# Edge values moved from the relu's scale into the destination one-hots, in a graph-attention kernel

## The reference, cut to what matters

```python
scores = jnp.sum(q[dst] * k[src], axis=-1) * scale
scores = scores + (edge_weight[:, None] @ we + be)[:, 0]
seg_max = jax.ops.segment_max(scores, dst, num_segments=n)
exp_s = jnp.exp(scores - seg_max[dst])
denom = jax.ops.segment_sum(exp_s, dst, num_segments=n)
attn = exp_s / jnp.maximum(denom[dst], 1e-12)
out = jax.ops.segment_sum(v[src] * attn[:, None], dst, num_segments=n)
```

## Time and profile before

| | us |
|---|---|
| median of 3 runs (1656.93 to 1661.5) | 1658.9 |
| the profiled execution | 1657.33 |
| its span in the trace | 1655.6 |

### The profile page before, as it was taken

How to read it: one execution, slowest core, us unless ns; L and a number is a source line. 1 busy time by engine, 2 the same in 40 slices (tenths; PEclk the granted TensorE clock), 3 DMA queues, 4 the chain that set the end, 5 groups by cost and what they waited for, 6 DMA issues and landing times.

```text
span 1655.6 us, 40803 instructions
## 1 busy us (share of the span) xinstructions
PE 1505.8 (91%) x9862; PEld 1311.8 (79%) x9862; DVE 1068.7 (65%) x2995; ACT 920.7 (56%) x2928; POOL 724.4 (44%) x1149
## 2 busy tenths in 40 slices
PE   5979999999999999995999999999999979974777
PEld 5968888988988988894888888888888869962444
DVE  7725888888888888885355544555455557985222
ACT  4748999999999999992333333333333334530111
POOL 0046777777777777771011101111011006752554
PEclk9989999999999999997999999999999989986988
DMA  8263444444444444446221122211221130124663
GB/s 190 41 181 78 111 108 112 110 109 113 108 111 110 108 112 109 110 112 154 84 77 67 67 82 84 72 66 71 84 83 67 53 77 28 61 69 117 189 184 99
DMA packets 220684, 164.30 MB, mean 99 GB/s; under 512 B 45888, under 2 KB 212749, under 8 KB 217412
## 3 DMA queue, kind: packets, MB, share of 16 engines
q1 hardware_dynamic: 189690, 96.79, 23.8%
q0 software_dynamic: 16544, 57.40, 10.0%
q10 hardware_dynamic: 14400, 9.55, 2.0%
HBM read 82.33 MB, written 85.50 MB: 101 GB/s over the span
## 4 chain that ended last, share of the span: by engine, by line
PE 65%; DVE 14%; issue 9%; DMA 4%; another core or an unknown queue 2%; ACT 2%; DVEq 2%; POOL 1%; ACTq 0%; POOLq 0%; SPq 0%
PE bank L1527 17%; PE bank L1494 13%; PE bank L1515 13%; DVE arena L1157 7%; DVE arena L1130 4%; PE bank L1534 4%; PE bank L1478 3%; PE bank L1559 3%; PE bank L1415 3%; PE bank L1567 3%; DMA arena<-rows_dram,arena 2%; DMA arena<-adj,gidx 1%; PE bank L1420 1%; PE bank L1422 1%
## 5 line engine op out<-in xcount | busy, mean ns | idle before, releaser
L833 ACT ACTIVATE arena<-bank,tables 128x128 f32<-128x128 f32 x2048 | 562.2, 375 | 43.6 <-PE bank L1478 42.9
L1494 PEld LDWEIGHTS bank<-arena 128*125 128x125 f32 x4096 | 536.4, 188 | 61.6 <-ACT arena L833 39.6
L1494 PE MATMUL bank<-arena 128*125 128x128 f32 x4096 | 559.3, 275 | 21.5 <-DVE arena L1130 9.6
L667 POOL TENSOR_SCALAR arena<-iota_row,held 128x125 f32<-128x125 f32 x768 | 464.8, 619 | 132.3 <-PE bank L1494 129.3
L1157 DVE SCALAR_TENSOR_TENSOR arena<-arena,tables,bank 125x128 f32<-125x128 f32 x1023 | 350.4, 342 | 93.9 <-DVE arena L1157 90.3
L859 ACT COPY arena<-bank 125x500 f32<-125x500 f32 (+1 forms) x175 | 90.7, 532 | 381.0 <-PE bank L1534 381.0
L1527 PE MATMUL bank<-V,arena 125*125 125x256 f32 x1250 | 296.4, 382 | 5.6 <-ACT arena L859 5.6
L1130 DVE TENSOR_TENSOR arena<-iota_row,tables 128x250 f32<-128x250 f32 x640 | 267.2, 418 | 9.0 <-issue 8.8
L1527 PEld LDWEIGHTS bank<-V,arena 125*125 125x125 f32 x1250 | 223.4, 188 | 38.0 <-ACT arena L859 10.3
L687 POOL COPY gidx<-arow 125x1 uint32 (+1 forms) x25 | 37.4, 1496 | 463.3 <-DVE wk_sb L1198 463.3
L1198 DVE CUSTOM_DVE_ANT_0 arena<-arena 125x3200 f32<-125x3200 f32 x25 | 87.3, 3494 | 222.5 <-ACT arena L842 222.5
(11 more groups left out here) (240 smaller groups left out, 1588.0 us busy)
## 6 DMA issues: line engine op xcount, KB each, us to landing
adj<-arena SPq DMA_DIRECT2D x256, 224.0 KB
adj<-arena SPq DMA_DIRECT2D x256, 26.0 KB
q_dram<-arena ACTq DMA_DIRECT2D x25, 125.0 KB
wq_sb<-q_dram SPq DMA_DIRECT2D x25, 125.0 KB, 7.9
rows_dram<-tables SPq DMA_DIRECT2D x25, 125.0 KB
rows_dram<-x SPq DMA_DIRECT2D x25, 125.0 KB
arena<-term_rows SPq DMA_DIRECT2D x192, 8.0 KB
V<-in_x SPq DMA_DIRECT2D x5, 560.0 KB
```

Source lines behind the costliest of these rows:

```text
L667: ins = nc.gpsimd.tensor_scalar(Xs[:, j % STAGES, k, :], iota_row[:, 0:TILE], held[:, h, c:c + 1], None, ALU.is_equal)
L833: ins = nc.scalar.activation(Ys[:, q, k, :], dist_bank(j)[:, k * LO:(k + 1) * LO], ACT.Relu, scale=nval_tab[:, bass.ds(i, 1)])
L1494: ins = mm(o, Xs[:, j % STAGES, k, :], Ys[:, j % STAGES, k, :], start=(k % SUB == 0), stop=(k % SUB == SUB - 1))
```

## The change

The value of an edge goes into X instead of Y. ScalarE copies both tables out of PSUM without a sign (`val_tab` in place of `nval_tab`). X is (iota == code) * value, in one TENSOR_SCALAR with two per-partition operands per chunk, on VectorE (L1130 before) and on GpSimd (L667). Y has no per-edge factor left, so one relu of 128x512 with the constant scale -1 makes the four chunks of a group. VectorE's TENSOR_TENSOR over two chunks becomes two TENSOR_SCALARs of one chunk each, and they are dealt out alternately: chunk 0 behind the sum k = 0, chunk 1 behind the sum k = 1 (chunks 0 and 2, 1 and 3 in VectorE's own groups). `held` holds codes and values and moves into the arena; its copy is 128x2x32.

```diff
-        code_tab, nval_tab = (tables[:, i * SLOTS * SUB:(i + 1) * SLOTS * SUB] for i in range(2))
+        edge_tabs = tables[:, 0:2 * SLOTS * SUB].rearrange("p (w n) -> p w n", w=2)
+        code_tab, val_tab = (edge_tabs[:, w, :] for w in range(2))
...
+        HELD = LOADG * GC
+        held = view(2 * 2 * HELD).rearrange("p (h w n) -> p h w n", h=2, w=2)
...
-        HELD = LOADG * GC
-        held = sb("held", [P, 2, HELD])
...
-                nc.gpsimd.tensor_copy(held[:, h, :], code_tab[:, bass.ds(n * HELD, HELD)]).then_inc(codes_held, 1)
+                nc.gpsimd.tensor_copy(held[:, h, :, :], edge_tabs[:, :, bass.ds(n * HELD, HELD)]).then_inc(codes_held, 1)
...
-                    ins = nc.gpsimd.tensor_scalar(Xs[:, j % STAGES, k, :], iota_row[:, 0:TILE], held[:, h, c:c + 1], None,
-                                                  ALU.is_equal)
+                    ins = nc.gpsimd.tensor_scalar(Xs[:, j % STAGES, k, :], iota_row[:, 0:TILE], held[:, h, 0, c:c + 1],
+                                                  held[:, h, 1, c:c + 1], ALU.is_equal, ALU.mult)
...
-                nc.scalar.mul(steps(nval_tab), ps[:, 1, :, :], -1.0).then_inc(tab_set, 1)
+                nc.scalar.copy(steps(val_tab), ps[:, 1, :, :]).then_inc(tab_set, 1)
...
-                for k in range(GC):
-                    i = g * GC + k
-                    ins = nc.scalar.activation(Ys[:, q, k, :], dist_bank(j)[:, k * LO:(k + 1) * LO], ACT.Relu,
-                                               scale=nval_tab[:, bass.ds(i, 1)])
-                ins.then_inc(y_ready, 1)
+                nc.scalar.activation(Ys[:, q, :, :], dist_bank(j)[:, 0:GC * LO].rearrange("p (k l) -> p k l", k=GC), ACT.Relu,
+                                     scale=-1.0).then_inc(y_ready, 1)
...
-                own = j % LOADG in OWN
-                if k and not own:
-                    return
-                cols = slice(k * SUB, (k + 1) * SUB)
-                ins = V_.tensor_tensor(Xs[:, s, cols, :], iota_row[:, 0:TILE].unsqueeze(1).to_broadcast([P, SUB, TILE]),
-                                       code_tab[:, bass.ds(g * GC + k * SUB, SUB)].unsqueeze(2).to_broadcast([P, SUB, TILE]),
-                                       ALU.is_equal)
-                if k == GROUP - 1 or not own:
+                for c in range(k, GC if j % LOADG in OWN else SUB, GROUP):
+                    i = g * GC + c
+                    ins = V_.tensor_scalar(Xs[:, s, c, :], iota_row[:, 0:TILE], code_tab[:, bass.ds(i, 1)], val_tab[:, bass.ds(i, 1)],
+                                           ALU.is_equal, ALU.mult)
+                if k == GROUP - 1:
                     ins.then_inc(x_ready, 1)
```

## The result

The changed kernel takes 1698.3 us (median; 1695.0 to 1701.4) against 1658.4 in the same comparison: a ratio of 1.024, with a 95% interval of 1.022 to 1.026. On another chip the pair gave 1698.8 and 1663.2, 1.021 (1.019 to 1.024). It is slower by some 40 us, inside the forecast range of 1650 to 1800, on the side forecast, and 19 us under the forecast time.

What follows compares the result with a forecast made beforehand. VectorE's beat was taken as the bound; partly barred chunks added 51 us over 30 turns and 7 in the plain turns, +58. With 1657.3 profiled that gave 1715, plus 1.6 to the median: 1717 us, range 1650 to 1800.

Steps and rivals of the forecast that it cites:

- The bound before: Kernel before: VectorE never waits for others, so its beat of 1.16 to 1.18 us per group bounds.
- ScalarE: One relu of 128x512 replaces the scaled relus: 0.6 us per group, gain 0 while VectorE bounds.
- VectorE's two chunks: Two one-hots in place of one on VectorE: 0.245 us from one start to the next, +9 us with nothing else changed.
- forecast, nothing barred: VectorE's halves without exclusion beyond today's: turn 19.3 us, +9 us, 1668; as a rival, chance 0.22.
- forecast with exclusion: VectorE's common halves partly barred by GpSimd: 0.605 us each, turn 20.8, +58 us; chance 0.32.
- The loop's end: End of each hardware-loop turn: 0.2 us added to the sixteen groups, as in the kernel before.
- Exclusion between GpSimd and VectorE: One-hots side by side: GpSimd bars VectorE's fast form part of the time, common half 0.605 us, +58 in all.
- The rival that followed it, 1763: VectorE's chunks wait until GpSimd's whole instruction ends: common half 0.665 us, +104 us, 1763; chance 0.22.
- GpSimd's own price: Second operand and multiplication on GpSimd's 619 ns one-hot: 0.05 to 0.1 us more, hidden; bounds 0 and +0.27.
- threshold of 0.77: GpSimd's one-hot stays hidden up to about 0.77 us, from 4.2 us free per turn.
- the rival in which it becomes the bound: GpSimd bounds by itself above 0.77 us per one-hot; at 0.89 a turn is 22.0 us, about 1756; chance 0.10.
- The signs named ahead: Expected in the profile after: chunk minimum near 0.33 us, longer GpSimd one-hots, ScalarE half busy, turn 20.8 us.

Runs made afterwards that it cites:

- easing VectorE in the common groups: Kernel before with VectorE's one-hots as single code-only chunks in common groups, old 250-column form in own groups: 1647.5 us, ratio 0.992.
- GpSimd eased: Changed kernel with GpSimd's one-hot comparing the code alone, its chunks' values left out: 1691.1 us, ratio 1.018 to the kernel before.
- the earlier wait: Kernel with values in VectorE's common chunks, its waits for next product and store moved ahead of the second sum's chunk: 1643.9 us, 0.989 of before.
- the run that eases both: Changed kernel with VectorE's old one-hot in its own groups and GpSimd's code-only one-hot, those values left out: 1644.8 us, 0.990 of before.

## Why the prediction was right or wrong, point by point

**The bound before: right.** VectorE's beat, with a latency of 0.22 to 0.25 us in each half that had no one-hot. Taking away half of ScalarE's work changed nothing (0.9994), easing VectorE in the common groups made it faster (0.992).

**ScalarE: right.** Gain 0; 597 ns against 0.6.

**VectorE's beat, halves on average** (us, from 160 to 728 us of each trace; the half over the loop's end apart):

| | first half, common | second half, common | over the loop's end | own group |
|---|---|---|---|---|
| before | 0.60 | 0.58 | 0.72 | 1.18 |
| forecast, nothing barred | 0.505 | 0.58 | 0.78 | 1.50 |
| forecast with exclusion | 0.605 | 0.605 | 0.80 | 1.51 |
| changed | 0.538 | 0.589 | 0.94 | 1.574 |
| GpSimd eased | 0.520 | 0.585 | 0.96 | 1.598 |

**VectorE's two chunks: right in kind, too small in size.** One chunk to the next instruction was priced at 0.245 us; the trace has 0.256 at the shortest (sum, chunk, sum in 0.512). The kernel with GpSimd eased shows this beat alone: 20.02 us a turn against my 19.3, +29 us of the run's time against +9. By the table a turn is 0.8 us longer than the first forecast row adds up to (19.2), and the terms that were mis-sized are the own groups (0.39 of it: they take 1.60, not 1.50), the common groups (0.24) and the loop's end (0.18). Of the 0.10 in each own group, 0.04 are the price of four chunks; the rest goes with chunks longer than their shortest. The loop's end was taken over from the kernel before as 0.2 (0.14 in the table) above another second half, and is 0.35 in the changed kernel and 0.375 with GpSimd eased; why is not shown.

**Exclusion between GpSimd and VectorE: this is the step that failed.** The forecast's +49 us above the plain beat rested on a common half of 0.605, with VectorE waiting for GpSimd's instruction: 1.21 for a common group. It is 1.127 with GpSimd never idle, against 1.085 with nothing barred, so a third of the term is there. The two do hold each other up, as the chunks with and without GpSimd beside them show (330 to 344 ns against 390). But none of the 1280 chunks of the changed kernel reaches a wait of 0.3 or more until a GpSimd instruction's end: the longest is 595 over a shortest of 329, and 6 are over 500. The median is 341. And it works both ways: GpSimd's one-hot is 836 on average over 782. Per turn that is 24 x 0.054 = 1.3 us of GpSimd's and 40 x 0.034 = 1.4 of VectorE's, but in VectorE's second halves the latency between sums, still 0.57 to 0.60, covers most of it, while GpSimd, which has no slack left, pays in full. Where the row went wrong: that L687 stood still for 1.6 us beside an instruction of 1.8 told the price of a long instruction. I used it for one of 0.33 us without scaling it. That the wait goes with the 0.065 us in which data is moved is a guess; no run varies that length.

The Trainium skill ("SBUF — State Buffer", Who interferes with whom) lets whichever comes second wait for the whole instruction of the first, with VectorE in its two-port mode. A block for the whole instruction shows in this case one way only, for L687 on GpSimd. By the rule, chunks beside a GpSimd that is busy all the time would wait up to 0.8 us each, and their median is 341 ns against a shortest of 329. The rival that followed it, 1763, is refuted.

**GpSimd's own price: the second step that failed.** I took 0.05 to 0.1, hidden below a threshold of 0.77, and gave the rival in which it becomes the bound one chance in ten, priced from 0.89. It is 0.195 alone, 0.12 for the multiplication and 0.08 for the second operand. At 0.785 it lands just past the threshold; the 54 ns of being held up beside VectorE take it further: 24 x 0.836, less the overlap of neighbours of 0.01 to 0.02, and two copies are the 20.2 us of a turn. The mechanism of that rival was right, and its chance was too low: with an upper bound of 0.27 over a slack of 0.15, nearly half of the open range lay past the point. The threshold itself was too generous: the kernel before with GpSimd's one-hot at 0.760 on average, under 0.77, is already 30 us slower (1692, one run), with VectorE's one-hot longer beside it.

**The time.** 1717 forecast, 1698 measured. It comes near by errors of opposite sign, which is luck: +49 for an exclusion of which a third is there, and against it VectorE's beat 20 us too short (9 for 29) and GpSimd's, which runs beside it, taken as hidden where it comes out as long. The range held for the right reason only in part. The sign was right for its first reason, that the fourth group gives back what three gain, but that reason was worth 9 us in my sum and 29 on the chip.

**The signs named ahead.** A shortest chunk near 0.33 us: 329. ScalarE at half: yes. GpSimd's one-hots longer than 619: yes, but 0.195 of the 0.217 is their own price, which I had at 0.1 or less. VectorE without waits for TensorE: yes. TensorE's waits: 20.3 us for L1126, the successor of L1130, as said, but the waits for ScalarE's relu, which were to vanish, are still there, 30.5 and 12.2 us for L832. A turn of 20.8: 20.16. Own groups longer than common ones: 1.57 against 1.13.

**What was left unused.** The alternation itself is good: with codes only in the common groups and the old form in the own groups the kernel is 0.8% faster than before, and with values in VectorE's common chunks and the earlier wait 1.1%. What makes the change slower is that it loads the two places without slack. In VectorE's own groups single chunks cost 14 us even with the code alone (1661.9 against 1647.5), and more with the value; and GpSimd's instruction takes the value too. With both taken back the kernel runs at 0.990 of before.

## What to carry to other kernels

Work taken from an engine that isn't the bound is worth nothing, and the place where it goes must have slack for it: price the second operand and the second operation on every engine that gets them, with the bounds beside that engine's idle time per turn, not its mean share. Idle time isn't free either: here 0.14 us more per instruction on GpSimd fitted into its idle time and still came with 0.04 us more on VectorE's one-hot and a kernel 30 us slower. When two engines end within 1% of each other, undoing either part alone shows next to nothing; only the run that eases both tells that both were bounds. A stall seen beside a long instruction is no price for a short one.

## What the runs showed of the hardware that I had not expected

- On GpSimd a TENSOR_SCALAR of 128x125 in fp32 takes, at the shortest, 590 ns with a comparison, 707 with a multiplication by a constant behind it, 782 to 787 with a multiplication by a per-partition operand.
- On VectorE it takes 270 ns at the shortest with a comparison and 329 with a multiplication by a second per-partition operand behind it, in kernels with a busy GpSimd 308 and 363 on average; the next chunk starts 0.19 and 0.25 us after it at the soonest.
- The two engines lengthen each other's instructions, but not by a whole instruction: VectorE's chunk takes 330 to 344 ns with GpSimd idle and 390 on average, up to 467, with GpSimd busy, in one and the same kernel.
- What GpSimd loses beside VectorE isn't told by VectorE's form alone. Where GpSimd never stops, it is 112 ns per instruction of 787 beside TENSOR_TENSORs with two SBUF inputs and 54 of 782 beside the TENSOR_SCALARs; where it has idle time, 29 of 590 to 53 of 707 beside the former and 25 of 591 to 41 of 594 beside the latter.
